# Two cross attentions of a two-layer block: projections started earlier, computed further ahead, and folded into the loop's own block

## What is computed

```python
# sublayer 1 (L0_xattn), 16 heads of 16
rq = (iQ @ Wq.T);  kv = (iK @ Wkv.T)                 # iK is the context, 1024 rows a batch
scores = einsum('bqhd,bshd->bhqs', rq, rk) / 4       # masked: -1e32
t = relu(scores + nbias)**2
attn = t / (t.sum(-1) + 1e-32)
x = x + einsum('bhqs,bshd->bqhd', attn, rv) @ Wo.T
# sublayer 4 (L1_xattn), 16 heads of 64: softmax attention over the same context
out = einsum('bhqk,bhkd->bhqd', softmax(q k^T / 8), v)
x = x + out @ w_o
```

## Time and profile before

| | us |
|---|---|
| median of 3 runs | 1034.07 |
| lowest and highest run | 1031.37, 1034.31 |
| the profiled execution | 1030.17 |
| its span (first to last instruction) | 1027.4 |
| PE busy in the span | 973.0 (95%) |
| mean granted TensorE clock | 0.983 |
| xattn0, span 0 to | 203.3 |
| xattn1's projections' block and its borders | 841.7 to 872.5 |

### The profile page before, as it was taken

One profiled execution on the slowest core, in us unless ns is written; L12 is line 12 of the kernel. 1 busy time (PEld: TensorE's weight loads), 2 busy tenths in 40 slices (PEclk: granted clock), 3 DMA queues, 4 the chain that ended last, 5 costly groups with the idle time before them and its releaser, 6 DMA issues. The chain is left out here.

```text
span 1027.4 us, 21006 instructions
## 1 busy us (share of the span) xinstructions
PE 973.0 (95%) x8776; PEld 805.2 (78%) x8776; DVE 554.1 (54%) x804; ACT 494.3 (48%) x708; POOL 163.8 (16%) x170
## 2 busy tenths in 40 slices
PE   8899999888799989899999999999999989979997
PEld 7688888665689975699999999999989976547554
DVE  4578777666444444665656564646565621386222
ACT  4677776353666635544454545444454420313221
POOL 2000000022134413012121211111111100420000
PEclk9999999899999999999999999999999999998999
DMA  5122110022023313111111111111130000999990
GB/s 152 45 66 64 46 49 3 9 56 64 26 77 93 92 46 119 42 42 41 42 42 41 41 41 41 41 41 41 41 122 0 1 1 1 268 338 291 285 300 20
DMA packets 55205, 81.40 MB, mean 79 GB/s; under 512 B 5201, under 2 KB 44578, under 8 KB 55138
## 3 DMA queue, kind: packets, MB, share of 16 engines
q1 hardware_dynamic: 55138, 80.43, 25.9%
HBM read 79.89 MB, written 0.52 MB: 78 GB/s over the span
## 5 line engine op out<-in xcount | busy, mean ns | idle before, releaser
L186 PE MATMUL ps<-f_pT_hi,f_cN_hi 128*128 128x256 f32 x512 | 145.4, 284 | 2.4 <-DVE f_pT_lo L1778 2.4
L186 PE MATMUL ps<-f_pT_hi,f_cN_lo 128*128 128x256 f32 x512 | 144.7, 283 | 0.0
L186 PE MATMUL ps<-f_pT_lo,f_cN_hi 128*128 128x256 f32 x512 | 144.7, 283 | 0.0
L1525 ACT ACTIVATE e_pr<-ps,e_negmax 128x1024 f32<-128x1024 f32 x64 | 71.5, 1117 | 129.8 <-DVE e_negmax L1530 127.6
L1778 DVE TENSOR_TENSOR f_pT_lo<-ps,f_pT_hi 128x1024 fp32r<-128x1024 f32 x64 | 78.3, 1223 | 82.1 <-ACT f_pT_hi L1726 82.1
L1726 ACT CAST f_pT_hi<-ps 128x1024 fp32r<-128x1024 f32 x64 | 65.0, 1015 | 84.9 <-PE ps L1815 84.8
L186 PE MATMUL ps<-e_cT_hi,e_qb_hi 128*128 128x512 f32 x256 | 105.6, 413 | 0.0
L409 DVE SCALAR_TENSOR_TENSOR a_u<-ps,a_floor,a_cap 128x1024 f32<-128x1024 f32 x64 | 79.2, 1280 | 45.9 <-PE ps L490 45.9
L186 PEld LDWEIGHTS ps<-f_pT_hi,f_cN_hi 128*128 128x128 f32 x512 | 97.8, 191 | 4.4 <-DVE f_pT_lo L1778 2.6
L186 PE MATMUL ps<-e_cT_hi,e_qb_lo 128*128 128x512 f32 x256 | 100.7, 393 | 0.0
L186 PE MATMUL ps<-e_cT_lo,e_qb_hi 128*128 128x512 f32 x256 | 99.8, 390 | 0.0
(11 more groups left out here) (379 smaller groups left out, 1990.4 us busy)
## 6 DMA issues: line engine op xcount, KB each, us to landing
k_w<-in_L_ffn_W SPq DMA_DIRECT2D x30, 1024.0 KB, 14.5
a_ctxT<-in_ctxT SPq DMA_DIRECT2D x16, 512.0 KB, 3.7
d_w<-in_L_ffn_w SPq DMA_DIRECT2D x32, 256.0 KB, 2.8
e_rawT<-in_ctxT SPq DMA_DIRECT2D x8, 1024.0 KB, 5.0
e_raw<-in_ctx SPq DMA_DIRECT2D x8, 1024.0 KB, 5.7
k_b<-in_L_ffn_b SPq DMA_DIRECT2D x14, 256.0 KB, 12.1
e_wq<-in_L_xattn_w_q SPq DMA_DIRECT2D x1, 1024.0 KB, 5.1
e_wk<-in_L_xattn_w_k SPq DMA_DIRECT2D x1, 1024.0 KB, 7.7
```

What stands on the lines that cost most here:

```text
L186: last = nc.tensor.matmul(out, a[i], b[j], start=start and n == 0, stop=stop and n == 2, skip_group_check=skip)
L1525: nc.scalar.activation(pr[:, p % NPR, :], core.ps[p % 2][:], ACT.Exp, bias=negmax[:, p:p + 1], accum_out=total[:, p:p + 1]).then_inc(exp_r ...
```

## The change

In `xattn0`:

- The pieces of the keys and values run three further ahead. Three of batch 1 stand before the loop, one ahead of the first scores and two behind, and each place computes the two that are three later; the last places of batch 6 have one piece and none.
- `split` and `remainder` of a batch move earlier by one place, `remainder(1, c)` ahead of `limits(0)`, `limits(b+1)` to j=2, and `normalize(b-1)` from j=0 to j=3.
- The first loads are cut: the key half of the weights, then the context in two halves of its columns, then the value half; each is split by itself and pieces 0 and 1 wait for the first half alone. Pieces 4 and 5 move ahead of the layernorm's transposes, and only the queries wait for the transposed x.
- A dummy square root on ACT stands first. 15 warm matmuls instead of 20.
- At the end `normalize` of the last batch works in two halves of the heads and the last projection waits for each; seven warm matmuls run ahead of it; the first half of x is added before it, with two of the next layernorm's bn_stats, which `memory0` then leaves out.

In `xattn1`: the projections' block is gone. Its value products run by pairs in the loop's block: two before the last batch's last `outputs`, two behind, and the projection of pairs p, p+1 between those of the pairs behind. The projection has one bank for each quarter. DVE adds quarter by quarter and makes all four bn_stats; five warm matmuls stand last. `attn1` leaves out the bn_stats and has 10 warm matmuls instead of 16. `oT` lies over the two raw context buffers.

```diff
-    def vector_stats(self, step, src):
+    def vector_stats(self, step, src, first=0):
-        for j in range(TT):
+        for j in range(first, TT):
             step(nc.vector.bn_stats(c.stats[:, j, :], src[:, j, :]), j == TT - 1)
...
+        AHEAD = 3
+        ahead = lambda b, j: [m for m in range(PIECES * (b + 1) + 2 * j + AHEAD, PIECES * (b + 1) + 2 * j + AHEAD + 2)
+                              if m < PIECES * B]
...
-            sp.dma_start(wkv[:], wkvT_d.rearrange("(c p) o -> p c o", p=P)).then_inc(wkv_in, 16)
-            for c in range(DC):
-                load_chunk(0, c)
+            sp.dma_start(wkv[:, :, 0:D], w_d[:, :, 0:D]).then_inc(wk_in, 16)
+            for h in range(2):
+                half = slice(512 * h, 512 * h + 512)
+                sp.dma_start(ctxT[:, :, half], ctxT_d[0, :, half].rearrange("(c p) s -> p c s", p=P)
+                             ).then_inc(ctx_in[h], 16)
+            sp.dma_start(wkv[:, :, D:2 * D], w_d[:, :, D:2 * D]).then_inc(wv_in, 16)
...
+            A.activation(dummy[:], ident[:, 0:1], ACT.Sqrt)
...
-                    if b + 1 < B:
-                        evict(b + 1, 2 * j)
-                        evict(b + 1, 2 * j + 1)
-                    if j in (1, 2) and b + 2 < B:
-                        split(b + 2, j - 1)
+                    for m in ahead(b, j):
+                        evict(m)
+                    if j == 0 and b + 2 < B:
+                        split(b + 2, 1)
+                    if j == 3 and b + 3 < B:
+                        split(b + 3, 0)
...
-                    if j == 0 and b > 0:
-                        normalize(b - 1)
-                    if j == 1 and b + 1 < B:
-                        limits(b + 1)
-                    if j in (2, 3) and b + 2 < B:
-                        remainder(b + 2, j - 2)
-            normalize(B - 1)
+                    if j < DC and b + 2 < B:
+                        remainder(b + 2, j)
+                    if j == 2 and b + 1 < B:
+                        limits(b + 1)
+                    if j == 3 and b > 0:
+                        normalize(b - 1)
+            residual(0)
+            dve.wait_ge(x_out, 1)
+            for j in range(2):
+                V.bn_stats(core.stats[:, j, :], x[:, j, :])
+            normalize(B - 1, 2)
+            residual(1)
...
-            for n in range(4):
-                piece(0, n)
-            norm.tensor(pe, 0)
-            for n in range(4, PIECES):
-                piece(0, n)
+            for m in range(6):
+                piece(m)
+            norm.tensor_turn(pe)
+            piece(6)
+            piece(7)
+            pe.wait_ge(norm.xnT, DC)
...
+            piece(PIECES)
             scores(0)
             scores(1)
+            piece(PIECES + 1)
+            piece(PIECES + 2)
...
             denominators(B - 1)
+            core.warm(0, 7)
             project(TT - 1)
...
+                    else:
+                        pe.wait_ge(v_in, 32)
+                        pe.wait_ge(exp_ready, HP * B)
+                        values(0)
+                        values(1)
                     outputs(b, 3, 0)
...
+                values(2)
+                values(3)
+                pe.wait_ge(pT_lo, HP * B)
+                pe.wait_ge(o_read, NG * B)
+                for p in range(0, HP - 2, 2):
...
+                    for j in range(TT):
+                        project(p, j)
+                    for j in range(TT):
+                        project(p + 1, j)
+                    if p + 4 < HP:
+                        values(p + 4)
+                        values(p + 5)
...
+                for j in range(TT):
+                    project(HP - 2, j)
+                    project(HP - 1, j).then_inc(y_psum, 1)
+                core.warm(0, 5)
```

More of the change, by code:

```diff
@@ L171, in tensor, with tensor_turn @@
         c.warm(7, warm)
+        self.tensor_turn(eng)
+        c.warm(7, between)
+        eng.wait_ge(self.xnT, DC)
+    def tensor_turn(self, eng):
+        c, nc = self.c, self.c.nc
         for j in range(TT):
@@ L177, in tensor @@
             last.then_inc(self.xnT_psum, 1)
-        c.warm(7, between)
-        eng.wait_ge(self.xnT, DC)
 def product3(nc, out, a, b, start, stop, skip=False):
@@ L301, in _, with split_first @@
             A = nc.scalar
+            def split_first(h, c):
+                half = slice(512 * h, 512 * h + 512)
+                act.wait_ge(ctx_in[h], 16)
+                A.copy(ctx_hi[0][:, c, half], ctxT[:, c, half]).then_inc(hi_ready, 1)
             def split(b, c):
@@ L342, in squares @@
                              scale=HD ** -0.5).then_inc(p_ready, 1)
[L344 to L348 removed]
+            act.wait_ge(ident_ready, 1)
+            A.activation(dummy[:], ident[:, 0:1], ACT.Sqrt)
+            act.wait_ge(wk_in, 16)
+            A.copy(wkv_hi[:, :, 0:D], wkv[:, :, 0:D]).then_inc(w_hi, 1)
+            for h in range(2):
+                for c in range(DC):
+                    split_first(h, c)
+            act.wait_ge(wv_in, 16)
+            A.copy(wkv_hi[:, :, D:2 * D], wkv[:, :, D:2 * D]).then_inc(w_hi, 1)
+            evict(0)
+            evict(1)
             norm.scalar_std(act)
[L350 to L351 removed]
+            for m in range(2, 6):
+                evict(m)
             norm.scalar_transposed(act)
[L353 to L354 removed]
             for c in range(DC):
                 split(1, c)
[L357 to L358 removed]
+            evict(6)
+            evict(7)
             for c in range(DC):
@@ L364, in _ @@
             queries(0)
+            evict(PIECES)
             act.wait_ge(w_in, 32)
             squares(0)
+            evict(PIECES + 1)
             squares(1)
+            evict(PIECES + 2)
+            split(2, 0)
             for b in range(B):
@@ L427, in _ @@
             norm.vector_transposed(dve)
+            for c in range(DC):
+                remainder(1, c)
             dve.wait_ge(w_in, 32)
@@ L430, in _ @@
             limits(0)
-            for c in range(DC):
-                remainder(1, c)
             clamp(0)
@@ L1770, in _ @@
                 each(act, B, batch)
+                for p in range(2, HP, 2):
+                    attended(p)
             @block.vector
@@ L1807, in _ @@
                 each(dve, B, batch)
+                for p in range(1, HP, 2):
+                    dve.wait_ge(v_psum, p + 1)
+                    nc.vector.tensor_copy(oT[:, p, :], core.bank(p % 4)).then_inc(oT_dve, 1)
+                for j in range(TT + 1):
+                    if j < TT:
+                        dve.wait_ge(y_psum, j + 1)
+                        nc.vector.tensor_tensor(x[:, j, :], x[:, j, :], core.bank(4 + j)[:, 0:D], ALU.add
+                                                ).then_inc(x_out, 1)
+                    if j >= 1:
+                        dve.wait_ge(x_out, j)
+                        nc.vector.bn_stats(core.stats[:, j - 1, :], x[:, j - 1, :]).then_inc(x_stats, 1)
+                dve.wait_ge(x_stats, TT)
             @block.tensor
@@ L1828, in outputs, with values, project @@
                     last.then_inc(o_psum, 1)
+                def values(p):
+                    if p >= 4:
+                        pe.wait_ge(oT_dve if p % 2 else oT_act, (p - 4) // 2 + 1)
+                    pe.wait_ge(o_read, NG * (B - 1) + p // 2 + 1)
+                    for g in range(2):
+                        h = 2 * p + g
+                        for c in range(DC):
+                            last = nc.tensor.matmul(core.bank(p % 4)[HD * g:HD * g + HD, :],
+                                                    wv[:, c, h * HD:(h + 1) * HD],
+                                                    qc[:, c, :, h * T:(h + 1) * T], start=c == 0, stop=c == DC - 1)
+                    last.then_inc(v_psum, 1)
+                def project(p, j):
+                    return nc.tensor.matmul(core.bank(4 + j)[:, 0:D], oT[:, p, j * P:(j + 1) * P], wo[:, p, :],
+                                            start=p == 0, stop=p == HP - 1)
                 def batch(b):
@@ L1895, in _ @@
                 for j in range(TT):
-                    for p in range(HP):
-                        last = nc.tensor.matmul(core.bank(4 + j // 2)[:, D * (j % 2):D * (j % 2) + D],
-                                                oT[:, p, j * P:(j + 1) * P], wo[:, p, :], start=p == 0,
-                                                stop=p == HP - 1)
-                    if j % 2:
-                        last.then_inc(y_psum, 1)
+                    project(HP - 2, j)
+                    project(HP - 1, j).then_inc(y_psum, 1)
+                core.warm(0, 5)
 def attn1(core, a, mixture):
```

150 lines of the change are left out of this document (69 added, 81 removed).

## The result

Four executions of the changed kernel took 1025.43 to 1026.65 us, median 1026.05, beside 1034.05 (1031.37 to 1034.31) of the kernel before. The ratio is 0.9938 with a 95% interval of 0.9912 to 0.9963. So the change is worth 6 to 8 us. The forecast was 1022, a gain of 12 against the median. The direction was right, the size too large, and the time stands near the upper end of the range.

The account below looks back on a forecast made before the run. PE, busy 95% of the span, was taken as the bound, leaving its idle and half-clock time and stage ends to win. Terms summed to -11.4 us: 1018.8 from the profile, 1022.7 from the median; forecast 1022, range 1017.5 to 1026.5.

Parts of the forecast that it names:

- Start: xattn0 up to the loop's first pieces: halved loads and pieces run ahead bring them to 31.9 instead of 36.57, -4.6 us.
- the wait of a piece on `evict`: Sign of being wrong in xattn0: the start gains under 4 us because a piece waits on `evict`.
- Places: xattn0's loop: outputs wait for the division moved to j=3, 0.1 us at each of five batches, +0.5 us (0 to 1).
- End of the pieces: xattn0, batch 6 j=2 to batch 7 j=1: 13.8 us instead of 14.8, -1.0 us (-1.5 to +2).
- my first rival: Clock falls where xattn0's pieces end; outputs, denominators and projection lose some 2 us: sum -9.4, time 1024; chance 0.28.
- two like cases: Before 32.85 and 199.31 PE was busy 1.2 of 5.3 us and 1 of 4, then ran slower; supports the clock rival.
- one gap of 2.36 us: xattn1 at 835.67: PE waits 2.36 us for the last probabilities; cited as a gap that did nothing to the clock.
- Tail: xattn0, last scores to x added: 12.3 us instead of 13.3 through division by halves, -1.0 us; 12.8 at clock 0.64.
- j=1 to j=2: Last batch of xattn0: division out of DVE's way, PE's 2.13 + 1.99 us remain of 4.25, -0.1 us.
- memory0: memory0's start: two bn_stats less, half of 1.41 us, -0.7 us.
- the slow case: memory0's 12 warm matmuls run at half clock and end last; its -0.7 us term then becomes nothing.
- xattn1: Second cross attention: value products fill waits of 2.36, 0.93 and 0.88 us, -4.2; root at 2.8 instead of 3.1, -0.3.

Follow-up runs that it names:

- experiment 1: Changed kernel with 12 empty matmuls in TensorE's two gaps at the end of the pieces (7 and 5); median 1024.57 us, ratio 0.9928 to the kernel before.
- experiment 3: Changed kernel with 14 instead of 10 empty matmuls at the start of attn1; median 1020.63 us, ratio 0.9910 to the kernel before.
- experiment 6: Changed kernel with xattn1's value products of pairs 4 to 7 in one run, all projections behind them; median 1022.21 us, ratio 0.9899 to the kernel before.
- experiment 7: Changed kernel with the division back at j=0 and 14 empty matmuls at attn1's start; median 1018.83 us, ratio 0.9860 to the kernel before.
- Experiment 2: Changed kernel with the division of batch b-1 put back from j=3 to j=0; median 1021.09 us, ratio 0.9892 to the kernel before.

## Why the prediction was right in direction and too large

- **Start (-4.6 forecast, -4.0 in the trace).** First matmul at 7.93 (8.0), no fall of the clock in the loop's first place. The missing 0.6 is the wait of a piece on `evict` behind the root (0.69), which I named as what would make me wrong and counted at nothing. In experiments 1, 3, 6 and 7, with x early, the start gained 5: the second place at 34.4 to 34.7 instead of 39.56.
- **Places (+0.5, +1.2).** The step was right, its size wrong: the outputs behind the division start 1.32 us behind the scores instead of 1.10, so it is 0.22 to 0.23 us a batch at five borders, where I had 0.1. Experiment 2 gives 1.10 back.
- **End of the pieces (-1.0, +1.8).** The step that failed is the last one of this count: "then 1.03, denominators 0.35 and projection 1.85", which took full clock for granted. These 3.2 us took 5.94, at a granted clock of 0.54. It was my first rival, at 0.28. I gave it 2 us, and it cost 2.7. The fall came in all five traces with both gaps open, and not in the one in which they were filled. The rival stood on the right rows, two like cases in the same trace, and the forecast had none on its side but one gap of 2.36 us that did no harm. That the clock fell is shown; which stillness of PE brought it down is not, since in four of the five traces it fell before the second gap (experiment 2). The clock page of the Trainium skill (TensorE: Matmul & The Clock Gate, What's actually happening) has full clock as what activity must earn. The trace agrees with that much: 0.54 from 176.90 to 184.40, behind a gap of 1.93 us.
- **Tail, j=1 to j=2, memory0 (-1.8, -2.2).** Right, with some luck in memory0. There the empty matmuls had run at half clock until 207 and held the transposes up until 207.83; in the changed kernel they ran at 1.0, so that the transposes came 2.9 instead of 4.5 us behind the block's start. The prediction had named the slow case only as what would make this term nothing.
- **xattn1 (-4.2 and -0.3, together -3.5).** All three waits are gone and the table's load is last before the root. What was missed is what a change between the two kinds of product costs, 0.8 of the missing 1.0, shown by experiment 6.
- **Behind the changed parts (0, +3.6).** For the fewer empty matmuls in attn1 the forecast had no term, that is, it put them at nothing without a reason; the first projection behind them took 8.64 us instead of 6.97, and 1.7 us were lost there. The rest, at the gate and ahead of the last stage, is the clock's own scatter: these lengths differ between two executions of one kernel.
- **Which execution to count from.** I summed up on a profile that was the fastest execution of its group and then took 1022, near what the sum gives from the median. Single executions of the kernel before lie anywhere from 1028.5 to 1035.4 us, so this choice alone moves the forecast by 4 us. That the time of 1026.05 lies inside the range owes something to it: from the profile the sum gave 1018.8, 7 us below.

## What to carry to other kernels

Work that is moved forward leaves a thin place where it would have been; write down how long TensorE stands still there and what follows, and cost that both at full and at half clock. Try to take away the wait before you fill it: moving one division back won 3 to 5 us (intervals that just overlap), more than half of it by waits that are gone whatever the clock does; filling the gaps with empty matmuls won 2.55 us in its place and nothing that could be told in the time. Where a queue holds copies that another engine waits for, put none of them behind an instruction that waits for a transfer.

## What the runs showed of the hardware

The clock's falls don't follow from the order of the instructions alone: with the same gap of 1.04 us it fell in five traces and not in three, behind the same gap of 1.93 us (experiment 2) within 1.3 us in four and not in six, and around ffn0's gate it stayed at half for 3.4 to 10 us. A fall that is avoided can be followed by one in a place that had none (204 to 208 in experiment 1). The time is therefore no plain sum of local gains, and a difference of 2 us between two single profiles says nothing until the granted clocks are laid side by side. The landing time of x, the fifth transfer issued, varied between two sets of traces by over 1 us (statistics at 10.0 to 11.1 or at 11.7 to 12.1). Two things stay open: why the fall in attn1 came in some executions with 10 matmuls and not in others, and why the clock held at the end of the pieces in every trace with the division at j=0, though TensorE's rows ahead were the same.
